# Two rows of the third sweep are begun inside the second, and the third sweep's rows come in another order

## What is computed

```python
# layer 0
fc_sc = values @ W + b
d_inv_sqrt = 1.0 / (jnp.sqrt(jnp.sum(adj, axis=1)) + 1e-8)
x = layernorm(x + (adj * d_inv_sqrt[:, None] * d_inv_sqrt[None, :]) @ fc_sc)
# layer 1
adj_hat = adj + eye
d_inv_sqrt = 1.0 / jnp.sqrt(jnp.sum(adj_hat, axis=1))
out = (adj_hat * d_inv_sqrt[:, None] * d_inv_sqrt[None, :]) @ (x @ W) + b
x = layernorm(x + relu(out))
```

## Time and profile before

| | |
|---|---|
| median of 3 runs | 1745.77 us (1744.44 to 1746.71) |
| the profiled execution's own time | 1744.39 us |
| its span, first to last instruction | 1742.6 us |
| PE busy, share of the span | 94% |
| DVE, ACT, POOL busy | 61%, 44%, 9% |
| DMA queues' share of 16 engines | 84% |

### The profile page before, as it was taken

How to read it: one execution, slowest core, us unless ns; L and a number is a source line. 1 busy time by engine, 2 the same in 40 slices (tenths; PEclk the granted TensorE clock), 3 DMA queues, 4 the chain that set the end, 5 groups by cost and what they waited for, 6 DMA issues and landing times. The chain is left out here.

```text
span 1742.6 us, 25481 instructions
## 1 busy us (share of the span) xinstructions
PE 1636.9 (94%) x10204; PEld 1458.6 (84%) x10204; DVE 1062.6 (61%) x1893; ACT 763.1 (44%) x904; POOL 164.6 (9%) x202
## 2 busy tenths in 40 slices
PE   0788989999999999989999999999999999999997
PEld 0688989999999999967888888888888877888885
DVE  2233233344355555587766665656466899999997
ACT  4332323232211100056554444444445777888885
POOL 0000000000000000211111000101010011111111
PEclk9999999999999999999999999999999999999999
DMA  9999999999999975368776666566575999999994
GB/s 384 420 421 420 420 420 412 420 420 418 419 418 419 378 314 231 103 231 303 257 282 224 245 227 228 200 259 244 182 261 228 420 418 419 420 419 418 420 416 172
DMA packets 88020, 580.77 MB, mean 333 GB/s; under 512 B 10816, under 2 KB 11072, under 8 KB 22368
## 3 DMA queue, kind: packets, MB, share of 16 engines
q1 hardware_dynamic: 76320, 541.23, 77.7%
q0 software_dynamic: 11584, 37.93, 5.8%
HBM read 560.22 MB, written 18.89 MB: 332 GB/s over the span
## 5 line engine op out<-in xcount | busy, mean ns | idle before, releaser
L783 PE MATMUL acc<-high,feat_high 128*128 128x512 f32 x1348 | 533.7, 396 | 12.5 <-DVE low L905 12.4
L785 PE MATMUL acc<-high,feat_low 128*128 128x512 f32 x1348 | 528.1, 392 | 0.0
L784 PE MATMUL acc<-low,feat_high 128*128 128x512 f32 x1348 | 528.1, 392 | 0.0
L905 DVE TENSOR_TENSOR low<-own,high 128x1024 fp32r<-128x1024 f32 x330 | 389.8, 1222 | 169.9 <-ACT high L802 168.2
L802 ACT CAST high<-own 128x1024 fp32r<-128x1024 f32 x330 | 337.1, 1053 | 200.1 <-PE acc L785 161.1
L758 PE MATMUL acc<-feat,lent 128*128 128x129 f32 x2880 | 332.9, 275 | 10.2 <-issue 10.2
L758 PEld LDWEIGHTS acc<-feat,lent 128*128 128x128 f32 x2880 | 327.3, 192 | 11.5 <-issue 11.5
L783 PEld LDWEIGHTS acc<-high,feat_high 128*128 128x128 f32 x1348 | 254.1, 188 | 70.5 <-issue 17.5
L785 PEld LDWEIGHTS acc<-high,feat_low 128*128 128x128 f32 x1348 | 253.7, 188 | 55.5
L784 PEld LDWEIGHTS acc<-low,feat_high 128*128 128x128 f32 x1348 | 254.1, 189 | 52.7
L905 DVE TENSOR_TENSOR low<-lent,high 128x1024 fp32r<-128x1024 f32 x182 | 211.9, 1220 | 7.3 <-ACT high L802 5.2
(11 more groups left out here) (89 smaller groups left out, 747.7 us busy)
## 6 DMA issues: line engine op xcount, KB each, us to landing
own<-adj_tiles SPq DMA_DIRECT2D x208, 1024.0 KB, 7.2
lent<-adj_tiles SPq DMA_DIRECT2D x181, 1024.0 KB, 16.0
lent_h<-adj_tiles SPq DMA_DIRECT2D x42, 1024.0 KB, 16.1
lent<-adj_far SPq DMA_DIRECT2D x42, 1024.0 KB, 18.1
lent_h<-adj_far SPq DMA_DIRECT2D x21, 1024.0 KB, 18.5
own<-adj_far SPq DMA_DIRECT2D x18, 1024.0 KB, 14.9
x_in<-x_rows POOLq DMA_DIRECT2D x32, 256.0 KB, 7.5
x_t<-x_cols SPq DMA_DIRECT2D x16, 256.0 KB, 15.3
```

Source lines behind the costliest of these rows:

```text
L783: nc.tensor.matmul(bank, f_high, a_high[:, chunk], start=(u == plan.first[g] and q == 0), stop=False)
L784: nc.tensor.matmul(bank, f_high, a_low[:, chunk], start=False, stop=False)
L785: mm = nc.tensor.matmul(bank, f_low, a_high[:, chunk], start=False, stop=(u == plan.last[g] and q == Q - 1))
L905: nc.vector.tensor_tensor(low(m), raw(n)[:, half * HALF:(half + 1) * HALF], high(m).bitcast(F32), ALU.subtract).then_inc(low_ready, 1)
```

## The change

In `loads`, each row i of sweep 2 is now followed by the tiles (15, i + 1) and, where it lies in that row, (14, i + 1) of sweep 3. So 15 tiles of row 15 and 14 tiles of row 14, 29 in all, are taken inside sweep 2, and (15, 0) and (14, 0) stay for sweep 3. The two rows' groups keep a PSUM bank each all through sweep 2, which leaves four of six for the others. The rest of sweep 3, 107 tiles, comes in a written-out order `REST3`, with (row, first column, last column) for each piece: rows 13 and 12 first, with rows 0, 15, 14 and 1 closed between pieces of rows 12 and 11. `turn_out` is one take earlier. What depended on "sweep 3" for the buffers MORE and for AHEAD now depends on the place before or after `last_late0`.

```diff
+BEGUN_ROWS = (15, 14)
+REST3 = [(13, 13, 0), (12, 12, 9), (0, 0, 0), (12, 8, 6), (15, 0, 0), (12, 5, 0), (11, 11, 8), (14, 0, 0), (11, 7, 5), (1, 1, 0), (11, 4, 0)] + \
+    [(r, r, 0) for r in (10, 2, 9, 3, 8, 4, 7, 5, 6)]
+ROWS3 = [i for i, _, last in REST3 if last == 0]
-        self.loads += [(2, i, j) for i in reversed(range(NB - 1)) for j in reversed(range(i + 1, NB))]
-        self.loads += [(3, i, j) for i in ROWS3 for j in reversed(range(i + 1))]
+        for i in reversed(range(NB - 1)):
+            self.loads += [(2, i, j) for j in reversed(range(i + 1, NB))]
+            self.loads += [(3, r, i + 1) for r in BEGUN_ROWS if r > i]
+        self.loads += [(3, i, j) for i, first, last in REST3 for j in range(first, last - 1, -1)]
...
-            self.turn_out[i] = self.empty[g] + 3
+            self.turn_out[i] = self.empty[g] + 2
...
-            ring = [(0, b) for b in range(RING)] + ([(sweep, b) for b in range(MORE)] if sweep == 3 or u <= last_late0 else [])
+            ring = [(0, b) for b in range(RING)] + ([(2 if u <= last_late0 else 3, b) for b in range(MORE)])
...
-            return k + AHEAD[self.loads[self.takes[k][0]][0]] if sub and k < self.end else k
+            return k + AHEAD[min(self.loads[self.takes[k][0]][0], 3 if k > last_late0 else 2)] if sub and k < self.end else k
```

More of the change, by code:

```diff
@@ L33 @@
 TURN_EVERY, TURN1_LAG, FEATURES1_LAG = 2, 3, 1
-ROWS3 = [r for k in range(NB // 2) for r in (NB - 1 - k, k)]
+BEGUN_ROWS = (15, 14)
+REST3 = [(13, 13, 0), (12, 12, 9), (0, 0, 0), (12, 8, 6), (15, 0, 0), (12, 5, 0), (11, 11, 8), (14, 0, 0), (11, 7, 5), (1, 1, 0), (11, 4, 0)] + \
+    [(r, r, 0) for r in (10, 2, 9, 3, 8, 4, 7, 5, 6)]
+ROWS3 = [i for i, _, last in REST3 if last == 0]
 ALU = mybir.AluOpType
@@ L110, in __init__ @@
             self.row_end.append(max(needed))
-        self.loads += [(2, i, j) for i in reversed(range(NB - 1)) for j in reversed(range(i + 1, NB))]
-        self.loads += [(3, i, j) for i in ROWS3 for j in reversed(range(i + 1))]
+        for i in reversed(range(NB - 1)):
+            self.loads += [(2, i, j) for j in reversed(range(i + 1, NB))]
+            self.loads += [(3, r, i + 1) for r in BEGUN_ROWS if r > i]
+        self.loads += [(3, i, j) for i, first, last in REST3 for j in range(first, last - 1, -1)]
+        assert len(set(self.loads)) == len(self.loads) and len(self.loads) == NB * NB * 2
         number = {key: n for n, key in enumerate(self.loads)}
```

## The result

The changed kernel takes 1757.35 us (median of 4 runs, 1756.04 to 1759.1) against 1746.24 us of the kernel before (4 runs): ratio 1.007, 95% interval 1.0057 to 1.0082. It is slower by 11.1 us, where 6.6 us were forecast. The profiled execution took 1756.83 us, where the prediction had 1751.0 us for it.

The account below looks back on a forecast made before the run. The prediction took PE as bound, busy 94% of 1742.6 us, with DVE near it in sweep 3. 1744.4 + 5.6 + 1 = 1751.0 us for the profiled execution, 1752.4 us for the median; range 1742 to 1762 us.

Parts of the forecast that it names:

- three slots: Rival, start of sweep 2: new one-layer tiles run at the slots' pace and open gaps; 1761 us, chance 0.14.
- term 1: Sweep 3: DVE becomes the bound; 12.6 us of stalls replace 5.6 us and 1.4 us of low clock, +5.6 us.
- the scaled and the unscaled sum: Sweep 3's forecast stalls: 14.9 us step by step, 12.5 us scaled by the method's earlier excess (5.6/6.7).
- The form of the stalls: Sweep 3: PE idle 1 to 2 us before `low` at nearly each row's end, some 12 us in all.
- at nothing: Effects counted as costing nothing: loads, row-end inputs issued by POOL, four PSUM banks, `turn_out` one take earlier.
- Term 2: Start of sweep 2: 8.6 us lost at the slots' pace against 7.5 us of gaps and low clock filled, +1 us.
- row ends hide: Rival: sweep 3's stalls vanish and the gaps at sweep 2's start are filled; 1731.3 us, chance 0.12.
- DMA relief at nothing: Sweep 3: 72 us of DMA leave a full stage without gain, only 0.25 us of idle PE being a load's.

Follow-up runs that it names:

- e1: The changed kernel with turn_out again three takes behind a row's last instead of two: 1756.54 us.
- e4: The changed kernel with the last normalisation's moments taken from one quarter of the row only, part of the computation left out: 1751.68 us.
- e7: The changed kernel with the same 29 tiles moved, but sweep 3's row ends spread to every 6 to 7 takes: 1753.48 us.
- e3: The kernel before, no tile moved, with sweep 3 reordered so that rows end every 7 to 9 takes instead of in pairs: 1741.91 us.
- e5: The kernel before with the last normalisation's moments taken from one quarter of the row only, part of the computation left out: 1739.65 us.
- e8: The changed kernel with the edits of e1 and e4 together: 1750.95 us.
- e2: The changed kernel with row 11's load of x put ahead of the store of row 12's sum in POOL's list: 1751.31 us.
- e6: The changed kernel with rows 15 and 14 begun only from row 8 of sweep 2 on, 18 tiles moved: 1749.04 us.
- e9: The changed kernel with the edits of e2 and e7 together: 1750.33 us.

## Why the prediction was right, and where it was not

The direction was right and 1757.35 us lies in the range of 1742 to 1762 us, but just outside the forecast's own 1748 to 1757 us, with 11.1 us for the 6.6 us forecast. That the range held it is in part luck: its upper end came from the pace of the three slots, and what filled the gap was something else.

- **Direction and term 1** (sweep 3, +5.6 us): right. The last part of the table has +6.6 us. That DVE's sum is the limit is shown by its 97 to 98% from 1480 us on with no waits of ACT for loads, by e1 (waits change place, time does not) and by e4 (a shorter end gains 5.6 us). e7 against e3 fits it but has a wait of its own, and that e5 gained almost as much as e4 does not fit the sizes. The sum of 12.6 us was near: 6.6 + 5.6 + 1.4, with the stalls of before and their clock which it replaces, are 13.6 us, between the scaled and the unscaled sum.
- **The form of the stalls** was half right. One per row end, yes, but half of each shows at the turn, since `turn_out` is one take earlier and `y_t` stands behind the `low` of that very take. I had this edit "at nothing", and e1 and e8 say that it is.
- **Term 2** (start of sweep 2, +1 us): mis-sized, +6.4 us, and its mechanism was wrong. It counted slots: 8.6 us lost at their pace, 7.5 us of gaps filled. The runs show a queue: the load of x for row 11 behind the store of row 12's sum, which waits until that row is finished. The step that failed is the one "at nothing" on row transfers, which follows POOL's list through sweep 3 only; its order in sweep 2 changes too. e2 puts two entries right and has 5.8 of the 6.4 us back, e6 all of it.
- **The rival "three slots"** falls with e2: eleven more one-layer tiles cost PE's own 2.72 us each within 0.6 us in sum.
- **The rival "row ends hide"** did not come. The Trainium skill (Perfetto Trace Analysis, Optimization Strategy) says that interleaving regimes may help; in this case it did not, 1757.35 against 1746.24 us. What was moved was PE's work into a stage with PE full, 533.3 us for 489.8 + 43.5; DVE's scarce time was in the row ends, which stayed.
- **DMA relief at nothing**: right for this kernel, since DVE was the limit; the waits in e4 say that loads stand right behind it.
- e3's gain of 2.4 to 3.4 us agrees with its trace: 4.9 us of idle time and 1.4 us of low clock are gone, and three new idle times of 3.1 us came, 3.2 us net.
- Open: how much of sweep 3's loss an order without the wait of e7 and e9 would give back, and whether loads are what kept e4 from its 9 us.

## What to carry to other kernels

When work is moved between stages, ask of each kind of work which engine is scarce there: a tile here gave DVE 0.45 us of lead, a row end took 3.78, so taking tiles away from the row ends made DVE the bound. Follow every engine's in-order list through the place where new work goes in, its DMA issues too: a load with nothing to wait for is as late as the store in front of it. If an engine's lead is what absorbs a burst, spacing the bursts is cheaper than moving work; that alone made the fastest full version here.

## What the runs showed of the hardware

The granted clock fell behind idle times that did not bring it down elsewhere. In the changed kernel two idle times of PE, of 1.19 us and, 1.13 us of work later, of 1.74 us, end at 752.8 us and were followed by a stretch at 0.50:

```profile
752.40:755.70 3.30, 2.94 (x7) 2.39 (x8) 3.30 (x4) 1.68 (x2) 0.53 (x1) 0.50 0.67 204
```

All eleven traces of this case have the same two idle times at this place, to 0.01 us. In seven of them the clock fell there (the changed kernel, e1, e2, e4, e5, e7, e8), in four it did not (the kernel before, e3, e6, e9). An idle time of 1.95 us brought no fall in the kernel before and one in e7. At 1.2 GHz PE did 7 to 9 instructions in 3.3 us instead of 15, so such a fall is worth some 1.5 us. Which idle times of 1.5 to 2.5 us bring it could not be told beforehand, and it differs between executions of the same work, so a difference of that size between two single traces may come from it alone.
